# A graph layer on one core: a column cleared behind every gather, and the narrow one-hots of the edge count made by ScalarE

## The chip, the cores and the metric

One core of one Trainium2 chip runs the kernel. Its engines are TensorE (PE, with weight loads PEld), VectorE (DVE), ScalarE (ACT), GpSimd (POOL) and SyncE (SP). The metric is the device time of one execution in microseconds; the median of several executions is compared. The profile is of one further execution.

## The reference, cut to what matters

6250 nodes with 256 features, 200,000 edges sorted by destination. The part that the change touches is the sum over edges.

```
h_neigh  = xn @ W_neigh
h_sparse = _maxk(h_neigh, 32)                 # keeps the 32 largest of a row
msg      = h_sparse[src]                      # a gather of 200,000 rows
summed   = segment_sum(msg, dst)              # added up by destination
deg      = segment_sum(ones, dst)
neigh    = summed / maximum(deg, 1)
gnn      = xn @ W_self + neigh
x        = x + gnn + mix(xn)                  # mix: linear attention with a gate
x        = x + ffn(layernorm(x))              # on the half of the rows with the largest weight
```

The layer norm, the attention, the gate and the closing network over the chosen rows are in the kernel too and are the same before and after.

## The kernel before

Nodes are cut into 50 tiles of 125. All engines' programs are written out by hand, joined by semaphores alone; nothing is scheduled by a tool. After a first stage (projection, the 32 largest, softmax sums; to about 266 us) comes the loop of 50 positions, one per tile of destinations, in an order set by a table `ORDER` before the program is built.

**Gathered tiles.** For 41 of the tiles GpSimd gathers the source rows of each edge from DRAM (`rows_d`, 512 fp16 each) with indirect DMAs of 128 rows. Four make a group, and `ring` holds eight groups; 232 groups make 928 gathers. Before a group GpSimd waits until PE has freed the slot (`s_slot_free`); SyncE waits for each group to land and tells PE (`s_landed`, line 588). For each group DVE makes a one-hot of destinations (line 1445), and PE adds the rows up with four matmuls of 512 columns and four of 2 (`visit`, lines 1057 and 1058).

**Dense tiles.** The first nine tiles have most edges. For them the kernel counts how often each pair of source and destination occurs, and then multiplies the count by the whole table (lines 1104, 1105). The count is taken in windows of ten destinations, 117 windows in all, and each window in units of at most 16 chunks of 128 edges. A chunk takes two one-hots on DVE, both by comparing `iota` with a column: a narrow one `lo` of 125 (the source within its tile, line 1461) and a wide one `key` of 500 (source tile and destination, line 1462). PE multiplies the two and adds up in one of two banks (line 1044); ACT takes a finished window out (line 874, "evacuation"). 978 chunks are counted, spread over the gathered tiles' positions, always at a position's end. Both one-hots lie in `count_hot`, 16 slots; `s_hot` tells that a chunk is made, `s_hot_free` and `s_counts` that PE has read it.

**A position, engine by engine.** PE: gate and projection matmuls, the visits, then `count` of its units. DVE: destination one-hots, `row_chain` of the position before (21 short steps), the count's one-hots, then sums. ACT: loads, `stage` (lines 821 and 822: it copies a unit's columns to `lo_staged` and `key_staged`), the gate's tanh (`gate_open`, line 812), the evacuations, the gate's gelu, stores. PE may not begin a window before ACT has emptied its bank:

```
if unit.first and unit.window >= 2:
    pe.wait_ge(s_evac, unit.window - 1)
```

`hold(engine, semaphore, value)` is a wait with an increment of a semaphore that nobody waits for.

## Time and profile before

| what | value |
|---|---|
| median of 3 runs | 2366.26 us (2359.95 to 2393.0) |
| the profiled execution, its own time | 2391.38 us |
| its span, first to last instruction | 2389.2 us |
| mean granted TensorE clock | 0.769 |
| busy | PE 1505.8, DVE 1297.9, ACT 288.7, POOL 1116.1 us |
| first and last gather | 266.1 and 2126.1 us |

A busy time counts an engine once however many instructions overlap. Idle time before a group of instructions is put down to what ended it; "remote" there, and "another core or an unknown queue" in the chain, mean that a semaphore was updated at a time at which no instruction of the profile ended. "issue" means that the engine waited for nothing that the profile shows.

### The profile page before, as it was taken

How to read it: one execution, taken by the hardware profiler on the slowest of the kernel's cores; microseconds unless marked ns; L12 is line 12 of the kernel's file. 1: busy time of each engine (PE TensorE's matmuls, PEld its weight loads, DVE VectorE, ACT ScalarE, POOL GpSimd, SP SyncE). 2: the span in 40 equal slices, each digit the busy share in tenths (PEclk: the TensorE clock that was granted, in tenths of full speed). 3: DMA queues.
4: the chain of work that ended last, by engine and by line, in shares of the span. 5: the costliest groups of instructions: out<-in, count | busy, mean ns of one | idle time of the engine just before them, and what ended most of it. 6: DMA issues, size and time to landing. Idle time of an engine off the chain costs nothing.

```text
span 2389.2 us, 29676 instructions
## 1 busy us (share of the span) xinstructions
PE 1505.8 (63%) x6995; PEld 945.6 (40%) x6995; DVE 1297.9 (54%) x4748; ACT 288.7 (12%) x764; POOL 1116.1 (47%) x1260
## 2 busy tenths in 40 slices
PE   2996545546655655765375666484748577653998
PEld 0553432223422422442243344352425354442666
DVE  6999624446754455555346546474555657475111
ACT  1443200000000000100001001011111111100211
POOL 2455646554656345445523644545353555342312
PEclk8998766667866776777677777786878677875999
DMA  8221333343433222323322322323232332231201
GB/s 172 67 77 60 111 91 102 84 112 95 124 86 96 65 78 85 90 65 87 91 64 75 95 80 79 100 76 89 72 91 78 88 111 72 81 91 47 71 18 29
DMA packets 128612, 199.87 MB, mean 84 GB/s; under 512 B 37596, under 2 KB 89643, under 8 KB 128510
## 3 DMA queue, kind: packets, MB, share of 16 engines
q0 software_dynamic: 53616, 131.54, 19.5%
q10 hardware_dynamic: 45176, 47.09, 7.3%
q1 hardware_dynamic: 29718, 20.03, 3.7%
q8 instruction: 45, 0.74, 0.1%
q14 instruction: 57, 0.47, 0.1%
HBM read 162.33 MB, written 35.71 MB: 83 GB/s over the span
## 4 chain that ended last, share of the span: by engine, by line
PE 30%; another core or an unknown queue 22%; DVE 21%; issue 18%; DVEq 3%; ACTq 2%; ACT 2%; SPq 1%; DMA 1%; POOL 0%; POOLq 0%
PE bank L1104 6%; DVE region_k L1462 5%; PE bank L1044 5%; DVE region_k L1461 5%; PE bank L1151 4%; PE bank L1165 3%; PE bank L1057 3%; PE bank L958 1%; PE bank L1030 1%; DVEq L1445 1%; ACTq L464 1%; DVE region_r L1346 1%; PE bank L1033 1%; DVE region_r L1342 1%
## 5 line engine op out<-in xcount | busy, mean ns | idle before, releaser
L719 POOL DMA_INDIRECT ring<-rows_d,stage x928 | 928.8, 1001 | 935.8 <-PE bank L1057 632.8
L1044 PE MATMUL bank<-region_k 128*125 128x500 f16 x978 | 407.9, 515 | 536.1 <-issue 216.8
L1461 DVE TENSOR_SCALAR region_k<-iota,region_k 128x125 f16<-128x125 f16 x978 | 281.6, 288 | 475.9 <-remote 408.2
L1044 PEld LDWEIGHTS bank<-region_k 128*125 128x125 f16 x978 | 156.8, 168 | 771.1 <-issue 352.0
L1462 DVE TENSOR_SCALAR region_k<-iota,region_k 128x500 f16<-128x500 f16 x978 | 350.9, 359 | 18.2 <-issue 17.8
L1057 PE MATMUL bank<-ring,region_v 128*125 x1084 | 315.2, 416 | 43.4 <-issue 43.3
L1445 DVE SCALAR_TENSOR_TENSOR region_v<-iota,tile_start,dstT 128x500 f16 x271 | 198.3, 740 | 77.6 <-issue 34.2
L874 ACT ACTIVATE region_k<-bank 125x500 f16<-125x500 f32 (+1 forms) x117 | 65.8, 578 | 1127.6 <-remote 852.6
L1057 PEld LDWEIGHTS bank<-ring,region_v 128*125 x1084 | 150.4, 139 | 126.8 <-issue 47.6
L1058 PE MATMUL bank<-ones,region_v 128*125 128x2 f16 x1084 | 182.4, 168 | 18.2 <-issue 17.7
L1058 PEld LDWEIGHTS bank<-ones,region_v 128*125 x1084 | 152.5, 141 | 29.7 <-issue 29.7
L1104 PE MATMUL bank<-region_r,region_k 125*125 125x512 f16 x450 | 140.7, 441 | 16.2 <-issue 16.2
L958 PE MATMUL bank<-region_r 128*125 128x512 f32 x200 | 96.7, 606 | 0.0
L1104 PEld LDWEIGHTS bank<-region_r,region_k 125*125 125x125 f16 x450 | 66.8, 148 | 54.9 <-issue 25.0
L1151 PE MATMUL bank<-region_k,region_v 128*128 128x500 f32 (+1 forms) x224 | 87.2, 548 | 1.4 <-DVE region_k L1670 1.4
L1165 PE MATMUL bank<-region_v,region_k 128*125 128x256 f32 x400 | 87.3, 379 | 0.0
L743 POOL DMA_INDIRECT out_dram<-region_r,region_v x24 | 28.6, 1190 | 125.8 <-DVE region_r L1690 122.1
L1105 PE MATMUL bank<-ones,region_k 125*125 125x2 f16 x450 | 77.4, 172 | 9.7 <-issue 9.6
L1165 PEld LDWEIGHTS bank<-region_v,region_k 128*125 128x125 f32 x400 | 74.6, 188 | 10.9
L691 POOL CAST region_r<-region_r 125x256 f16<-125x256 f32 x50 | 25.1, 502 | 114.3 <-DVE region_r L1350 112.7
L1553 DVE TENSOR_SCALAR col_deg<-bank 125x1 f32<-125x1 f32 x50 | 7.7, 154 | 129.7 <-PE bank L1109 112.4
L1030 PE MATMUL bank<-region_v 128*125 128x256 f32 x200 | 75.4, 513 | 0.0
(307 smaller groups left out, 1988.8 us busy)
## 6 DMA issues: line engine op xcount, KB each, us to landing
ring<-rows_d,stage POOLq DMA_INDIRECT x928
kept_d<-region_v ACTq DMA_DIRECT2D x50, 252.0 KB
region_v<-xT_d ACTq DMA_DIRECT2D x53, 125.0 KB
xT_d<-region_r ACTq DMA_DIRECT2D x51, 125.0 KB, 2.0
rows_d<-region_r SPq DMA_DIRECT2D x50, 125.0 KB
region_k<-in_x_dram ACTq DMA_DIRECT2D x50, 125.0 KB
out_dram<-region_v ACTq DMA_DIRECT2D x50, 125.0 KB
region_v<-in_x_dram SPq DMA_DIRECT2D x5, 1120.0 KB
```

Of the source, the lines that this page charges most:

```text
L719: pool.indirect_dma_start(out=ring[:, c, :], out_offset=None, in_=rows_d, in_offset=bass.IndirectOffsetOnAxis(ap=stage[:, c:c + 1], axis=0 ...
L958: m = pe.matmul(bank[1 + s % 2][0:T, :], xT[:, s % 2, k * T:(k + 1) * T], wkv[:, k, :], start=(k == 0), stop=(k == KC - 1))
L1030: pe.matmul(p_sum, xTc[:, turn, k * T:(k + 1) * T], w_self[:, k, :], start=(k == 0), stop=False)
L1044: m = pe.matmul(out, lo, key, start=(c == WINDOW_AT[unit.window]), stop=(c + 1 == WINDOW_AT[unit.window + 1]))
L1057: m = pe.matmul(total, onehot_s, row_s, start=False, stop=False, skip_group_check=True)
L1058: d = pe.matmul(deg_sum, onehot_s, ones16[:], start=False, stop=False, skip_group_check=True)
L1104: pe.matmul(total, counts16[:, b, :], table[:, b, :], start=False, stop=False, skip_group_check=True)
L1151: m = pe.matmul(up_bank(n)[:, 0:wide], w1[:, k, n * 128:(n + 1) * 128], x3T[:, g % 2, k, 0:wide], start=(k == 0), stop=(k == KC - 1))
L1165: m = pe.matmul(y_pair(h)[:, u % 2, :], hid[:, g % 2, n, u * T:(u + 1) * T], w2[:, n, :], start=(n == 0), stop=(n == NH - 1))
L1445: dve.scalar_tensor_tensor(out=part(hot_bytes, HOT, SLOT_HOT, hot, 0, SLOT_HOT).bitcast(F16).rearrange("p (a t) -> p a t", a=GC), in0=iota ...
L1461: dve.tensor_scalar(lo, iota[:, 0:T], lo_staged[:, at, u:u + 1], None, ALU.is_equal)
L1462: dve.tensor_scalar(key, iota[:, 0:KEYS], key_staged[:, at, u:u + 1], None, ALU.is_equal).then_inc(s_hot, 1)
```

## The change

It has two parts.

1. Behind every gather GpSimd sets one column of a new small tile `pause` to zero. The last clear of a group raises `s_pause`, and before each round of eight groups GpSimd waits for the clears of the round before.
2. The narrow one-hot is no longer made by DVE. ACT makes it in two steps: |iota - lo| per chunk (Abs with the negated column as bias), and Relu(1 - that) over up to eight chunks (`PIECE`) at once, in place, after a wait for its own Abs (`s_far`). `s_lo` tells PE. The narrow ones get 32 slots (`lo_hot`), the wide ones 12 (`key_hot`).

With the second part ACT's order changes: staging stands behind the gate's tanh and is interleaved with the low halves, and the evacuation of a window behind the low halves of the next unit.

```diff
-    COUNT_HOT = 16
+    KEY_HOT = 12
+    LO_HOT = 32
+    PIECE = 8
...
+    PIECES_OF = []
+    for unit in UNITS:
+        before = sum(len(pieces) for pieces in PIECES_OF)
+        PIECES_OF.append([Piece(before + p, unit.at + offset, min(PIECE, unit.chunks - offset))
+                          for p, offset in enumerate(range(0, unit.chunks, PIECE))])
...
+        pause = sb("pause", [128, RING * GC])
...
+            pool.sem_inc(s_pause, 1)
...
                         done = (r + BLOCKS[block][0]) * ROUNDS + j
+                        hold(pool, s_pause, done * RING + 1)
...
                                     in_offset=bass.IndirectOffsetOnAxis(ap=stage[:, c:c + 1], axis=0)).then_inc(s_land[block][q], 16)
+                                paused = pool.memset(pause[:, c:c + 1], 0.0)
+                            paused.then_inc(s_pause, 1)
...
-                act.activation(lo_staged[:, unit.number % STAGED, 0:unit.chunks], src_lo[:, bass.ds(at, unit.chunks)], ACT.Copy)
+                act.activation(lo_staged[:, unit.number % STAGED, 0:unit.chunks], src_lo[:, bass.ds(at, unit.chunks)], ACT.Copy,
+                               scale=-1.0)
...
+            def low(unit):
+
+                act.wait_ge(s_staged, unit.number + 1)
+                for piece in PIECES_OF[unit.number]:
+                    if piece.at + piece.chunks > LO_HOT:
+                        free(act, piece.at + piece.chunks - 1 - LO_HOT)
+                    for c in range(piece.at, piece.at + piece.chunks):
+                        last = act.activation(lo_slots(c), iota[:, 0:T].rearrange("p (a t) -> p a t", a=1), ACT.Abs,
+                                              bias=lo_staged[:, unit.number % STAGED, c - unit.at:c - unit.at + 1])
+                    last.then_inc(s_far, 1)
+                    act.wait_ge(s_far, piece.number + 1)
+                    ends = min(piece.chunks, LO_HOT - piece.at % LO_HOT)
+                    for first, chunks in ((piece.at, ends), (piece.at + ends, piece.chunks - ends)):
+                        if chunks:
+                            last = act.activation(lo_slots(first, chunks), lo_slots(first, chunks), ACT.Relu, bias=ones[:, 0:1],
+                                                  scale=-1.0)
+                    last.then_inc(s_lo, 1)
...
+                act.wait_ge(s_m3, n + 2)
+                gate_open(n + 1)
+                closed = []
                 for unit in at.units:
                     stage(unit)
-                act.wait_ge(s_m3, n + 2)
-                gate_open(n + 1)
...
+                    low(unit)
+                    while closed:
+                        evacuate(closed.pop(0))
                     if unit.last:
...
+                        closed.append(unit.window)
+                while closed:
+                    evacuate(closed.pop(0))
...
-                    lo, key = hot_slot(c)
+                    if c == unit.at or PIECE_OF[c] != PIECE_OF[c - 1]:
+                        pe.wait_ge(s_lo, PIECE_OF[c] + 1)
                     pe.wait_ge(s_hot, c + 1)
...
-                    if c >= COUNT_HOT:
-                        free(c - COUNT_HOT)
-                    dve.tensor_scalar(lo, iota[:, 0:T], lo_staged[:, at, u:u + 1], None, ALU.is_equal)
-                    dve.tensor_scalar(key, iota[:, 0:KEYS], key_staged[:, at, u:u + 1], None, ALU.is_equal).then_inc(s_hot, 1)
+                    if c >= KEY_HOT:
+                        free(dve, c - KEY_HOT)
+                    dve.tensor_scalar(key_slot(c), iota[:, 0:KEYS], key_staged[:, at, u:u + 1], None, ALU.is_equal).then_inc(s_hot, 1)
```

The order on GpSimd before, at the head of a round of the gathers:

```order
L708 ISA
L176 ISA [waits s_slot_free]
L719 DMA ring<-rows_d,stage 128x512 [waits s_stage0]
L719 DMA ring<-rows_d,stage 128x512 x3
L176 REGISTER_ALU
L719 DMA ring<-rows_d,stage 128x512 [waits s_slot_free]
```

and the same place now:

```order
L734 ISA
L186 ISA [waits s_pause,s_slot_free]
L746 DMA ring<-rows_d,stage 128x512 [waits s_stage0]
L749 MEMSET pause 128x1
L746 DMA ring<-rows_d,stage 128x512
L749 MEMSET pause 128x1
```

Each of the four gathers of a group has a memset behind it, and the head of a round waits for `s_pause` as well as for the slot.

On ACT before, the staging of the last of three units of a position, the gate's tanh (L812) and the three evacuations:

```order
L821 ISA [waits s_hot]
L821 ACTIVATE region_k<-region_k 128x6
L822 ISA
L822 ACTIVATE region_k<-region_k,win_start 128x6
L812 ACTIVATE region_v<-bank 128x250 [waits s_m3]
L874 ACTIVATE region_k<-bank 125x50x10 [waits s_counts] x2
L874 ACTIVATE region_k<-bank 125x50x5 [waits s_counts]
L809 ACTIVATE hgT<-region_v,bg 64x125 [waits s_hgpre]
```

and now the same position from its tanh (L841) through the low halves of its first unit, of nine chunks; L850 and L852 stage, L862 is the Abs and L869 the Relu:

```order
L841 ACTIVATE region_v<-bank 128x250 [waits s_m3]
L477 TENSOR_LOAD bounds
L477 ISA x2
L850 ISA [waits s_hot]
L850 ACTIVATE region_k<-region_k 128x9
L852 ISA
L852 ACTIVATE region_k<-region_k,win_start 128x9
L862 ACTIVATE region_k<-iota,region_k 128x125 [waits s_hot_free,s_staged]
L862 ACTIVATE region_k<-iota,region_k 128x125 x7
L869 ACTIVATE region_k<-region_k,ones 128x8x125 [waits s_far]
```

The tanh has moved ahead of all staging, and a unit's staging, Abs and Relu now stand together; the evacuation of its window comes only behind those of the next unit.

On DVE before, the end of `row_chain` and the first chunks of the count:

```order
L1516 TENSOR_SCALAR w_all<-col_w,br 125x1 [waits s_step5]
L1517 TENSOR_SCALAR region_v<-col_w,br 125x1
L1461 TENSOR_SCALAR region_k<-iota,region_k 128x125 [waits s_step6,s_hot_free,s_staged]
L1462 TENSOR_SCALAR region_k<-iota,region_k 128x500
L1461 TENSOR_SCALAR region_k<-iota,region_k 128x125 [waits s_hot_free]
```

and now:

```order
L1562 TENSOR_SCALAR w_all<-col_w,br 125x1 [waits s_step5]
L1563 TENSOR_SCALAR region_v<-col_w,br 125x1
L1516 TENSOR_SCALAR region_k<-iota,region_k 128x500 [waits s_step6,s_hot_free,s_staged]
L1516 TENSOR_SCALAR region_k<-iota,region_k 128x500 [waits s_counts]
L1516 TENSOR_SCALAR region_k<-iota,region_k 128x500 [waits s_hot_free] x7
```

Only the wide one-hots are left, each with its wait for a free slot. In the built program ACT has 978 Abs and 183 Relu more, DVE 978 one-hots less.

## Rows read from the trace of the kernel before

**Rows 1.** The page: busy time of each engine, and the chain by engine.

```profile
PE 1505.8 (63%) x6995; PEld 945.6 (40%) x6995; DVE 1297.9 (54%) x4748; ACT 288.7 (12%) x764; POOL 1116.1 (47%) x1260
...
PE 30%; another core or an unknown queue 22%; DVE 21%; issue 18%; DVEq 3%; ACTq 2%; ACT 2%; SPq 1%; DMA 1%; POOL 0%; POOLq 0%
```

**Rows 2.** The page's costliest groups: busy us, mean ns, then idle time before and releaser.

```profile
L719 POOL DMA_INDIRECT ring<-rows_d,stage x928 | 928.8, 1001 | 935.8 <-PE bank L1057 632.8
L1044 PE MATMUL bank<-region_k 128*125 128x500 f16 x978 | 407.9, 515 | 536.1 <-issue 216.8
L1461 DVE TENSOR_SCALAR region_k<-iota,region_k 128x125 f16<-128x125 f16 x978 | 281.6, 288 | 475.9 <-remote 408.2
...
L874 ACT ACTIVATE region_k<-bank 125x500 f16<-125x500 f32 (+1 forms) x117 | 65.8, 578 | 1127.6 <-remote 852.6 <-PE bank L1044 204.7 <-issue 70.3
```

**Rows 3.** Busy time by stretch: PE, PEld, DVE, ACT, POOL, granted clock, DMA share, GB/s.

```profile
1318.30:1327.70 9.40, 5.42 (x16) 1.75 (x14) 6.94 (x29) 0.00 (x0) 7.27 (x8) 0.80 0.36 99
1327.70:1338.10 10.40, 1.29 (x3) 0.36 (x2) 0.00 (x0) 0.00 (x0) 7.91 (x9) 0.50 0.37 109
1338.10:1341.40 3.30, 0.00 (x0) 0.00 (x0) 0.00 (x0) 0.00 (x0) 0.00 (x0) 0.50 0.14 40
```

**Rows 4.** Timeline around that burst: start, us, engine, instruction, [idle before <-releaser].

```profile
1314.48 0.21 ACT L821 ACTIVATE region_k<-region_k 128x7 f32 x1 [0.35 <-issue]
...
1318.38 1.90 PE L1044 MATMUL bank<-region_k 128*125 128x500 f16 x5
...
1326.44 0.57 PE L1044 MATMUL bank<-region_k 128*125 128x500 f16 x1 [1.10 <-DVE region_k L1462]
...
1330.68 0.57 PE L1044 MATMUL bank<-region_k 128*125 128x500 f16 x1 [0.83 <-issue]
...
1337.11 0.94 POOL L719 DMA_INDIRECT ring<-rows_d,stage  x1 [0.30 <-issue]
...
1341.41 0.26 DVE L1461 TENSOR_SCALAR region_k<-iota,region_k 128x125 f16<-128x125 f16 x1 [13.77 <-remote]
1341.61 1.07 ACT L874 ACTIVATE region_k<-bank 125x500 f16<-125x500 f32 x2 [26.46 <-remote]
1342.26 3.18 PE L1044 MATMUL bank<-region_k 128*125 128x500 f16 x7 [11.00 <-ACT region_k L874]
```

**Rows 5.** Busy time by stretch, columns as in rows 3: three other stretches with gathers.

```profile
585.80:590.80 5.00, 5.00 (x13) 2.08 (x12) 5.00 (x25) 0.59 (x1) 4.12 (x3) 0.57 0.29 80
...
633.90:640.80 6.90, 6.66 (x28) 3.60 (x26) 6.90 (x32) 0.59 (x1) 5.39 (x5) 0.96 0.34 99
1583.10:1593.20 10.10, 7.59 (x25) 3.93 (x24) 10.10 (x49) 2.95 (x5) 8.30 (x6) 0.82 0.28 78
```

**Rows 6.** Timeline of PE and POOL in the first two of these stretches.

```profile
584.51 11.82 PE L1044 MATMUL bank<-region_k 128*125 128x500 f16 x28 [2.35 <-DVE region_k L1462]
585.76 1.39 POOL L719 DMA_INDIRECT ring<-rows_d,stage  x1 [0.30 <-issue]
587.46 1.39 POOL L719 DMA_INDIRECT ring<-rows_d,stage  x1 [0.31 <-issue]
...
631.81 9.78 PE L1044 MATMUL bank<-region_k 128*125 128x500 f16 x33
```

**Rows 7.** Timeline of POOL at the start: memsets behind a DMA and among memsets.

```profile
6.61 0.57 POOL L643 DMA_DIRECT2D br<-in_L_ffn_br_dram  x1
7.16 0.24 POOL L644 MEMSET ident<- 128x128 f32 x1
...
11.22 0.09 POOL L666 MEMSET eps<- 125x1 f32 x1
```

**Rows 8.** Line 719, the gathers: ns least/median/most, first and last start.

```profile
L719 POOL DMA_INDIRECT ring<-rows_d,stage x928: 940/947/1717, 266.1 to 2126.1; - x186
```

**Rows 9.** ACT's groups from 400 to 2130 us: busy us, mean ns, idle before.

```profile
L822 ACT ACTIVATE region_k<-region_k,win_start 128x6 f32 (+10 forms) x123 | 35.7, 290 | 0.4 <-issue 0.4
...
L812 ACT ACTIVATE region_v<-bank 128x250 f32<-128x250 f32 x49 | 18.1, 370 | 183.5 <-PE bank L1025 114.7 <-remote 63.0 <-issue 5.7
```

More of the change, by code:

```diff
@@ L127, in build @@
             UNITS.append(Unit(len(UNITS), w, offset, held, WINDOW_AT[w] + offset, offset == 0, offset + held == chunks))
+    Piece = namedtuple("Piece", "number at chunks")
+    PIECES_OF = []
[3 more added lines that the diff above has]
+                          for p, offset in enumerate(range(0, unit.chunks, PIECE))])
+    PIECE_OF = {c: piece.number for pieces in PIECES_OF for piece in pieces for c in range(piece.at, piece.at + piece.chunks)}
     Spot = namedtuple("Spot", "dense tile units since")
@@ L214, in build @@
         counts16 = region_k.take([T, NT, T + 1], F16)[:, :, 0:T]
-        count_hot = region_k.take([128, COUNT_HOT, LW + KEYS], F16)
+        lo_hot = region_k.take([128, LO_HOT, LW], F16)
+        key_hot = region_k.take([128, KEY_HOT, KEYS], F16)
         lo_staged = region_k.take([128, STAGED, UNIT])
@@ L515, in agg_bank, with lo_slots, key_slot, free @@
             return bank[(0, 4)[at.n % 2]][0:T, :]
-        def hot_slot(c):
-            return count_hot[:, c % COUNT_HOT, 0:T], count_hot[:, c % COUNT_HOT, LW:LW + KEYS]
+        def lo_slots(c, chunks=1):
+            return lo_hot[:, c % LO_HOT:c % LO_HOT + chunks, 0:T]
+        def key_slot(c):
+            return key_hot[:, c % KEY_HOT, :]
+        def free(engine, c):
+            closed = sum(c >= end - 1 for end in WINDOW_AT[1:])
+            if c + 1 in WINDOW_AT:
+                engine.wait_ge(s_counts, closed)
+            else:
+                engine.wait_ge(s_hot_free, c + 1 - closed)
         def h_psum(s):
@@ L854, in store_row, with evacuate @@
                 act.dma_start(out_t[:, at.tile:at.tile + 1, :], rowbuf[:, u:u + 1, C:2 * C]).then_inc(s_rowout[u], 16)
+            def evacuate(window):
+                k = window % NW
+                wide = min(WIN, T - k * WIN)
+                act.wait_ge(s_counts, window + 1)
+                act.activation(counts16[:, :, k * WIN:k * WIN + wide],
+                               count_bank(window).rearrange("p (d h) -> p h d", h=NT)[:, :, 0:wide], ACT.Copy).then_inc(s_evac, 1)
             def position(at):
@@ L1041, in count @@
                 for c in range(unit.at, unit.at + unit.chunks):
-                    lo, key = hot_slot(c)
+                    if c == unit.at or PIECE_OF[c] != PIECE_OF[c - 1]:
+                        pe.wait_ge(s_lo, PIECE_OF[c] + 1)
                     pe.wait_ge(s_hot, c + 1)
-                    m = pe.matmul(out, lo, key, start=(c == WINDOW_AT[unit.window]), stop=(c + 1 == WINDOW_AT[unit.window + 1]))
+                    m = pe.matmul(out, lo_hot[:, c % LO_HOT, 0:T], key_slot(c), start=(c == WINDOW_AT[unit.window]), stop=(c + 1 == WINDOW_AT[unit.window + 1]))
                     m.then_inc(s_counts if c + 1 == WINDOW_AT[unit.window + 1] else s_hot_free, 1)
```

17 lines of the change are left out of this document (2 added, 15 removed).

## Prediction, made before the changed kernel had run

> **What bounds the kernel now.** I read the page's totals and chain first [rows 1]. No engine is full: PE is busy 63% of 2389.2 us, DVE 54%, POOL 47%. The chain that ended last is put down to "another core or an unknown queue" for 22% and to "issue" for 18%, although this kernel has one core. So two fifths of the path are waits that no finished instruction explains, and the question is where they lie.
>
> The costliest groups say where [rows 2]. PE sits idle 536.1 us before the 978 count matmuls (L1044), DVE 475.9 us before the 978 narrow one-hots (L1461), nearly all of it "remote", and ACT 1127.6 us before the 117 evacuations (L874). POOL sits idle 632.8 us before its gathers for PE to free a ring slot. All four wait for each other in the count phase.
>
> One position shows how. A burst of some 20 gathers runs from 1312.6 to 1338.1 [rows 3, 4]. From 1327.7 to 1338.1 PE is busy 1.29 of 10.4 us, DVE and ACT not at all, and only POOL works; for another 3.3 us after the burst nothing works. The single instructions are plainer [rows 4]: PE ends its 14th count at 1331.25, so the window whose seven chunks came first was complete long before, yet ACT starts its two evacuations at 1341.61 and DVE its next one-hot at 1341.41, both "remote". Finished work is told late. What coincides is the gathers, issued one behind the other with 0.30 us between: 0.95 + 0.30 = 1.25 us each.
>
> Other stretches have gathers and no such silence [rows 5, 6]. At 585.76 gathers of 1.39 us start 1.70 apart, and PE runs 28 counts without a gap (11.82 us). From 1583.1 to 1593.2, six gathers in 10.1 us, DVE is busy all the time and PE 7.59 us. From 633.9 to 640.8, five gathers in 6.9 us or 1.38 each, PE is busy 6.66 us, in a run of 33 counts. But from 1318.3 to 1327.7 [rows 3], eight gathers begin in 9.4 us (1.25 to 1.39 apart), and PE already waits up to 1.10 us for a one-hot long made [rows 4]. So signals pass freely at 1.7 us, hardly at 1.25, and either way in between. Cause and effect are not separable here: the longer gathers are also those beside which DVE works.
>
> **The clears.** Each of 928 gathers gets a memset of one column behind it. The nearest row is the 125x1 memset: 0.09 us, and a memset started 0.02 us before the POOL DMA ahead of it ended, without a gap of its own [rows 7]. So 928 x 0.09 = 84 us on POOL. It lies on the path as far as the burst does, which I take as all of it. The lower bound is 0, where POOL waits for a slot anyway (632.8 us [rows 2]). The upper bound is a second 0.30 us gap behind each clear: 928 x 0.39 = 362 us. I take 84, since the row of a memset behind a DMA is the nearest. The new wait on the clears stands once per 32 gathers, 28 times after the first; the group's gathers are queued behind it, then SP's forwarding of landings and PE's visits. If the clear's own signal is prompt it costs the drained queue, some 1 us, between 0 and the 3.3 us that signals took after the burst [rows 3]: 28 us, at most 92.
>
> What the clears give back is the disputed term. They part two gathers by 1.25 + 0.09 = 1.34 us at least, between the bad and the good stretch. Bounds: nothing, or all 536.1 us of PE's idle time before counts [rows 2]. I take half, 268 us.
>
> **The narrow one-hots.** DVE loses 978 instructions of 288 ns, 281.6 us [rows 2]. DVE is idle in the stalls, so this gives nothing by itself while the stalls stand; what it gives is less traffic beside the gathers. Those have median 947 and mean 1001 ns [rows 2, 8], so 928 x 54 ns = 50 us is stretch by DVE's work. With one of two one-hots gone I take half of it back, 25 us (bounds 0 and 50). The Trainium skill, "SBUF — State Buffer", section "Who interferes with whom", says that a DVE instruction in a two-port mode and a GpSimd instruction exclude each other for their whole length and that no other pair contends. The trace agrees on the first half (gathers of 1.39 beside one-hots, 0.95 alone); the second half leaves the late signals unexplained.
>
> ACT gains 978 Abs of 128x125 and 183 Relu, in the built program, of up to 8x125. Its nearest rows [rows 2, 9]: 290 ns for six elements with a bias column, 370 ns for 250 and 578 ns for 500 elements, so 208 / 250 = 0.83 ns an element. An Abs lasts 290 + 119 x 0.83 = 389 ns; two evacuations took 1.07 us together [rows 4] where one lasts 0.58 to 0.59, so 0.11 overlaps and the pitch is 0.28 us: 274 us. The Relus: 978 x 125 x 0.83 ns = 101 us, and 183 x 0.2 = 37 us to start. Together 412 us, 0.42 us a chunk. PE counts at 0.42 us a chunk (11.82 us for 28) at a granted clock of 0.57, near the lower of its levels, and at 0.30 (9.78 us for 33) at 0.96 [rows 5, 6]. In the 10 us of visits ACT runs ahead by up to 32 chunks, so at the low clock the low halves cost nothing. If PE no longer stalls and the clock stays high, ACT sets the pace: up to 978 x 0.12 = 117 us, which is the lid on a full release; I put none of it on the half release. ACT also waits for itself before each group of Relus; that wait and the signal to PE are two more that can come late. "ScalarE: Activation LUTs", section "Rules for kernel authors", of the Trainium skill speaks against this move (Relu and simple arithmetic belong on VectorE) and gives 0.3 us plus 0.83 ns an element: an estimate by it is 978 x 0.404 + 183 x 0.3 + 101 = 551 us. The trace agrees on the slope. ACT was busy 288.7 us of 2389.2, so either sum fits.
>
> The stages now stand behind the tanh of the gate, and each behind the low halves of the unit before. DVE's wide one-hots of the second unit thus wait some 7 x 0.42 = 2.9 us more, while PE counts the first. Key slots go from 16 to 12; PE had counted 14 when it stopped [rows 4], so DVE stops two chunks earlier in a stall. An evacuation stands behind the next unit's low halves; PE needs it only a unit later. I cost all three at nothing under the cover of the visits and of the first unit's counts; without it, 2.9 us in each of some 40 counting positions is 116 us, the reason why I take half and not more.
>
> **The sum** against the profiled execution (2391.38 us around a span of 2389.2): -268 + 84 + 28 - 25 = -181, so 2210. That execution lies 25 us over the median of 2366.26, so 2185; I say 2190.
>
> **The rivals.** *Full release.* Nothing comes late any more: 2391 - 536 + 84 + 28 - 25 + 117 = 2059, in the median 2034. POOL is no obstacle: 928 x 1.34 = 1244 us against the 1860 us from its first gather to its last [rows 8]. For it: 28 and 33 counts without a gap beside gathers. Against: the trace's good stretches are all ones in which DVE works without pause.
>
> *Slower: the burst only gets longer.* Signals hang on the gathers being in flight, not on the distance at which POOL issues them; the silence lasted 3.3 us beyond the last gather [rows 3], which a gap on POOL does not explain. Then each burst of some 20 grows by 20 x 0.09 = 1.8 us, and behind each come the same 3.3 us. Price: 84 + 28 us, and up to 2 us of late self-waits of ACT per position, about 20 us: 2391 + 132 = 2523, in the median 2498; with the Relus' signals hidden 2478. It decides if PE still stands idle 10 us before an evacuation.
>
> *No difference: the lock alone.* The distance at which gathers pass signals is set by DVE's work beside them, and the clears only make up for the one-hots taken away: 84 + 28 - 50 = +62, less some 60 us of stalls that 1.34 instead of 1.25 us relieves: 2391 + 2, in the median 2368. The row for it is the stretch from 1318.3 to 1327.7 [rows 3]. The skill's port rule, read strictly, gives this case.
>
> *The change does not do what it says* is thin: nobody reads the cleared tile, but the memset occupies POOL all the same.
>
> **Chances.** Half release (2090 to 2315) 0.42; full release (below 2090) 0.15; no difference (2320 to 2413) 0.16; slower 0.27. 2% of 2366 is 47 us, about what a measurement can tell from nothing; so faster 0.57, same 0.16, slower 0.27. The range leaves out the lower half of the full release and the tail of the slower case: 2035 to 2480.
>
> **What would show it.** In the new profile: (1) starts of gathers 1.34 us apart in bursts when DVE is idle; 1.6 or more means a second gap. (2) PE's idle time before counts, 536 now, near 270; near zero is the full release, unchanged the slower case. (3) "remote" ahead of the evacuations and of DVE's one-hots halved. (4) ACT's Abs near 0.39 us, in pitch 0.28, ACT busy near 700 us. (5) Mean gather below 1001 ns. (6) POOL's wait for PE (632.8) shrunk: whoever is late next is POOL itself, or ACT's low halves ahead of PE's counts. The forecast is wrong if the distance between gathers has nothing to do with the late signals, or if a clear costs far more than a memset among memsets.

## The result and the profile after

The changed kernel takes 2498.17 us in the median of four runs (2469.2 to 2519.12); the kernel before took 2369.61 us in four runs beside it. The ratio is 1.047, interval 1.039 to 1.055. It is below the ratio of the two medians (1.054) since it leaves out executions over 1.5% longer than the fastest of their kernel; the one profiled here, and those profiled in e3, e8 and e16 below, are of that kind. Forecast were 2190 us and a range of 2035 to 2480: the wrong direction, and the median is 18 us outside the range. The profiled execution took 2519.12 us around a span of 2517.1.

The page of the changed kernel: totals, the chain by engine, and the costliest groups (busy, mean ns of one, then the engine's idle time before them and what ended most of it).

```profile
span 2517.1 us, 30984 instructions
PE 1446.7 (57%) x6995; PEld 941.7 (37%) x6995; DVE 1145.0 (45%) x3770; ACT 732.5 (29%) x1925; POOL 1189.7 (47%) x2188
...
PE 31%; another core or an unknown queue 27%; DVE 15%; issue 14%; ACT 8%; DVEq 3%; SPq 1%; ACTq 1%; DMA 0%; POOL 0%; POOLq 0%
...
L746 POOL DMA_INDIRECT ring<-rows_d,stage x928 | 891.4, 961 | 985.4 <-PE bank L1113 756.1
L1100 PE MATMUL bank<-region_k 128*125 128x500 f16 x978 | 365.9, 507 | 757.0 <-ACT region_k L869 262.2
L1516 DVE TENSOR_SCALAR region_k<-iota,region_k 128x500 f16<-128x500 f16 x978 | 297.2, 373 | 805.6 <-remote 415.9
...
L862 ACT ACTIVATE region_k<-iota,region_k 128x125 f16<-128x125 f16 x978 | 300.5, 388 | 60.5 <-PE bank L1100 56.4
L908 ACT ACTIVATE region_k<-bank 125x500 f16<-125x500 f32 (+1 forms) x117 | 66.4, 571 | 850.1 <-remote 691.7
...
L869 ACT ACTIVATE region_k<-region_k,ones 128x1000 f16<-128x1000 f16 (+7 forms) x183 | 153.7, 853 | 5.5 <-ACT region_k L862 0.3
...
L749 POOL MEMSET pause<- 128x1 f32 x928 | 115.5, 124 | 0.3
```

Against [rows 1, 2]: PE's idle time before the counts (L1044, now L1100) rose from 536.1 to 757.0 us, the wait of the gathers for PE from 632.8 to 756.1, and the unexplained share of the chain from 22 to 27%. The mean gather fell from 1001 to 961 ns. The clears (L749) cost POOL 115.5 us of busy time. The view of line L746 gives the first and last start; before they were 266.1 and 2126.1 [rows 8]:

```profile
L746 POOL DMA_INDIRECT ring<-rows_d,stage x928: 940/946/1719, 265.7 to 2249.3; - x186
```

The gathering stretch is 124 us longer, the rest of the program 4 us. One burst of it in the timeline of all engines (start, length, engine, line, tiles, and in brackets the idle time ahead of it):

```profile
1380.78 0.95 POOL L746 DMA_INDIRECT ring<-rows_d,stage  x1 [0.19 <-issue]
...
1381.71 0.12 POOL L749 MEMSET pause<- 128x1 f32 x1
1381.97 0.58 PE L1088 MATMUL bank<-region_v 128*125 128x256 f32 x1 [1.50 <-issue]
1382.03 0.95 POOL L746 DMA_INDIRECT ring<-rows_d,stage  x1 [0.19 <-issue]
1382.97 0.12 POOL L749 MEMSET pause<- 128x1 f32 x1
1383.28 0.94 POOL L746 DMA_INDIRECT ring<-rows_d,stage  x1 [0.19 <-issue]
...
1384.07 0.58 PE L1088 MATMUL bank<-region_v 128*125 128x256 f32 x1 [1.51 <-issue]
...
1389.00 0.37 PE L1074 MATMUL bank<-region_v 128*128 128x125 f32 x1 [1.05 <-issue]
1390.41 0.95 POOL L746 DMA_INDIRECT ring<-rows_d,stage  x1 [0.19 <-issue]
1391.10 0.37 PE L1074 MATMUL bank<-region_v 128*128 128x125 f32 x1 [1.74 <-issue]
...
1393.99 0.16 DVE L1599 TENSOR_SCALAR col_deg<-bank 125x1 f32<-125x1 f32 x1 [20.01 <-remote]
...
1394.23 0.59 ACT L908 ACTIVATE region_k<-bank 125x500 f16<-125x500 f32 x1 [23.14 <-remote]
```

Three things stand here. Gathers start 1.25 us apart (1380.78, 1382.03, 1383.28), just as before: the gap of 0.30 us is now 0.12 us of clear and 0.19 of rest. And the silence is the same: DVE waits 20.01 us and ScalarE 23.14 us, until 3 us behind the last gather, while PE starts one matmul in 1.4 to 2.1 us. And the matmuls that PE starts so slowly have no wait in the program between them (L1088 twice, then L1074): late signals of other engines can't hold them. A count over the whole trace says the same of matmuls that follow one of their own line with no wait between: from the seventh distance on in a row of gathers (each begun under 1.30 us after the last) PE stands idle 284 ns before them on average (61 matmuls), elsewhere 6 ns (1785). So "finished work is told late" is a part of what happens: PE's own next step can be late as well. The windows of the same burst show it in sums (us, busy time of each engine, granted clock):

```profile
1382.00:1391.40 9.40, 2.75 (x6) 1.43 (x5) 0.00 (x0) 0.00 (x0) 7.34 (x14) 0.50 0.36 99
```

DVE and ACT do nothing in 9.4 us, PE is busy 2.75 us of them at the lower level of its clock (0.50). New is a wait inside the count phase, in the view of waits of DVE (in all, times, longest):

```profile
DVE region_k L1516 <- remote: 415.9, 24, 36.1
DVE region_k L1516 <- ACT region_k L852: 222.4, 38, 25.1
```

In the kernel before DVE waited 7.5 us for the same staging. PE's waits before the counts changed hands, too. Before and after:

```profile
PE bank L1044 <- ACT region_k L874: 161.0, 14, 21.2
PE bank L1044 <- DVE region_k L1462: 131.4, 101, 19.1
```
```profile
PE bank L1100 <- ACT region_k L869: 262.2, 21, 25.4
PE bank L1100 <- DVE region_k L1516: 257.8, 35, 29.5
```

PE no longer waits for an evacuation (the wait for L874 has no counterpart for L908), but for the Relus that make the narrow one-hots, and twice as long for the wide ones.

### The profile page after: what moved, and what is told of

It reads as the page before. It is cut to its first block, busy times and chain, and to the rows that moved or that the text cites. A ratio compares the mean times of both kernels' runs of the same rounds, so it can differ in the third digit from the quotient of the medians.

```text
span 2517.1 us, 30984 instructions
## 1 busy us (share of the span) xinstructions
PE 1446.7 (57%) x6995; PEld 941.7 (37%) x6995; DVE 1145.0 (45%) x3770; ACT 732.5 (29%) x1925; POOL 1189.7 (47%) x2188
## 4 chain that ended last, share of the span: by engine, by line
PE 31%; another core or an unknown queue 27%; DVE 15%; issue 14%; ACT 8%; DVEq 3%; SPq 1%; ACTq 1%; DMA 0%; POOL 0%; POOLq 0%
PE bank L1100 6%; PE bank L1160 5%; DVE region_k L1516 4%; ACT region_k L862 4%; PE bank L1207 3%; PE bank L1221 3%; PE bank L1113 3%; PE bank L1085 2%; ACT region_k L869 2%; PE bank L1074 1%; PE bank L1013 1%; PE bank L1088 1%; PE bank L1068 1%; DVEq L1501 1%
## 5 line engine op out<-in xcount | busy, mean ns | idle before, releaser
L746 POOL DMA_INDIRECT ring<-rows_d,stage x928 | 891.4, 961 | 985.4 <-PE bank L1113 756.1
L1100 PE MATMUL bank<-region_k 128*125 128x500 f16 x978 | 365.9, 507 | 757.0 <-ACT region_k L869 262.2
L1516 DVE TENSOR_SCALAR region_k<-iota,region_k 128x500 f16<-128x500 f16 x978 | 297.2, 373 | 805.6 <-remote 415.9
L1100 PEld LDWEIGHTS bank<-region_k 128*125 128x125 f16 x978 | 160.2, 173 | 940.8 <-issue 610.6
L862 ACT ACTIVATE region_k<-iota,region_k 128x125 f16<-128x125 f16 x978 | 300.5, 388 | 60.5 <-PE bank L1100 56.4
L908 ACT ACTIVATE region_k<-bank 125x500 f16<-125x500 f32 (+1 forms) x117 | 66.4, 571 | 850.1 <-remote 691.7
L869 ACT ACTIVATE region_k<-region_k,ones 128x1000 f16<-128x1000 f16 (+7 forms) x183 | 153.7, 853 | 5.5 <-ACT region_k L862 0.3
L749 POOL MEMSET pause<- 128x1 f32 x928 | 115.5, 124 | 0.3
L841 ACT ACTIVATE region_v<-bank 128x250 f32<-128x250 f32 x51 | 19.3, 379 | 310.2 <-PE bank L1080 257.1
```

The source lines that it names most:

```text
L746: pool.indirect_dma_start(out=ring[:, c, :], out_offset=None, in_=rows_d, in_offset=bass.IndirectOffsetOnAxis(ap=stage[:, c:c + 1], axis=0 ...
L862: last = act.activation(lo_slots(c), iota[:, 0:T].rearrange("p (a t) -> p a t", a=1), ACT.Abs, bias=lo_staged[:, unit.number % STAGED, c - ...
L869: last = act.activation(lo_slots(first, chunks), lo_slots(first, chunks), ACT.Relu, bias=ones[:, 0:1], scale=-1.0)
L1100: m = pe.matmul(out, lo_hot[:, c % LO_HOT, 0:T], key_slot(c), start=(c == WINDOW_AT[unit.window]), stop=(c + 1 == WINDOW_AT[unit.window + 1]))
L1516: dve.tensor_scalar(key_slot(c), iota[:, 0:KEYS], key_staged[:, at, u:u + 1], None, ALU.is_equal).then_inc(s_hot, 1)
```

## The experiments

Every ratio is to the kernel before, timed on the same chip (its medians were 2371 to 2421 us). The first four expectations name times for a chip on which it takes 2370; theirs took 2421, so I compare ratios. I add a count worked out from the starts of the 928 gathers in each trace: how many times eight gathers in a row began within 9.0 us. I call this a **close train**, counted anew from every gather, so a long row holds several; the kernel before has 250, the changed one 402 in the profile above. Seven distances of over 1.29 us can't make a close train, so for five and ten clears the 0 only repeats that gathers start 1.33 or 1.47 us apart.

| kernel | ratio [95%] | PE idle before counts, us | close trains |
|---|---|---|---|
| one clear (e1) | 0.988 [0.979, 0.996] | 523.1 | 226 |
| low halves on ScalarE, no clear (e2, e16) | 1.026 [1.017, 1.035]; 1.049 [1.032, 1.065] | 633.0; 719.2 | 483; 506 |
| ScalarE's staging late (e3) | 1.002 [0.994, 1.011] | 576.7 | 283 |
| five clears (e4) | 0.871 [0.865, 0.878] | 132.5 | 0 |
| the changed kernel (e5, e17) | 1.052 [1.041, 1.062]; 1.058 [1.047, 1.069] | 697.3; 722.7 | 400; 395 |
| changed, staging early (e6) | 1.032 [1.022, 1.041] | 685.6 | 364 |
| changed, five clears (e7) | 0.904 [0.896, 0.911] | 277.8 | 0 |
| three clears (e8) | 0.937 [0.927, 0.947] | 408.1 | 69 |
| changed, five clears, no Relu (e9) | 0.894 [0.887, 0.901] | 258.6 | 0 |
| ten clears (e10) | 0.875 [0.871, 0.879] | 30.8 | 0 |
| changed, five clears, staging early (e11) | 0.893 [0.888, 0.898] | 253.3 | 0 |
| five increments (e12) | 0.877 [0.872, 0.881] | 109.8 | 60 |
| ten increments (e13) | 0.896 [0.888, 0.905] | 10.4 | 0 |
| five waits (e14) | 1.020 [1.008, 1.033] | 587.2 | 249 |
| twenty increments a group (e15) | 0.880 [0.873, 0.886] | 95.0 | 64 |
| eleven waits (e18) | 0.878 [0.874, 0.883] | 105.4 | 65 |

### The parts of the change alone

**One clear.** The kernel before with `pause`, `s_pause`, the wait at the head of a round and

```
                                    in_offset=...).then_inc(s_land[block][q], 16)
+                                paused = pool.memset(pause[:, c:c + 1], 0.0)
+                            paused.then_inc(s_pause, 1)
```

> The kernel before with the clears behind the gathers and the wait on them once a round; both one-hots stay on DVE. Theory A (the clears are innocent: in the profile after, gathers still started 1.25 us apart, so each clear of 0.12 us lies inside the gap of 0.30 us that was there before): 2340 to 2395, gathers 1.25 apart, PE idle before the counts some 536 us as before. Rival B (the clears cost a gap of their own or their wait does, and are the loss): 2450 to 2500. Rival C (the clears do free the signals, as forecast, and ScalarE's part ate more than they gave): under 2300, PE idle before the counts under 450 us.

Measured 0.988: theory A, with gathers still 1.25 us apart. The clear and its wait cost nothing on balance and give 1.2%.

**The low halves alone.** The changed kernel without the lines above.

> The changed kernel without the clears and their wait; ScalarE makes the narrow one-hots. Theory A (all of the loss is in ScalarE's part): 2465 to 2530, PE idle before the counts some 750 us. Rival B (the clears are the loss): near 2370. Rival C (the clears helped and ScalarE's part cost more than the loss seen): above 2530.

Measured 1.026, half of the loss at first sight. A later comparison moved that (below).

**The order alone.** In `position` of the kernel before:

```
-                for unit in at.units:
-                    stage(unit)
                 act.wait_ge(s_m3, n + 2)
                 gate_open(n + 1)
+                for unit in at.units:
+                    stage(unit)
```

> The kernel before with one thing of the change: ScalarE stages the indices of a position's units behind the gate's tanh instead of ahead of the wait for the projection. No clears, DVE makes both one-hots. Theory A1 (ScalarE's staging now comes late, and DVE's one-hots with it: in the profile after DVE stands idle 222 us for the staging, in 38 stretches): a good part of the loss, 2420 to 2490, and DVE idle for the staging some 150 us or more. Theory A2 (the loss is in the extra signals and work of the low halves, not in the order): 2350 to 2390, since DVE has other work until then.

Measured 1.002, and DVE waits 9.3 us for the staging: A2. Behind the tanh alone it comes in time.

**Both parts, and the staging put back.** The changed kernel again, and the changed kernel with `stage` of all units ahead of `act.wait_ge(s_m3, n + 2)` and only `low` behind it.

> The changed kernel once more, on the chip of the three beside it, since chips differ by 2% (before took 2370 on one, 2421 on another). By the ratios so far of the two parts alone (clears 0.988, ScalarE's low halves 1.026) the sum of both would be 1.014, by the first comparison 1.047. Theory A (the parts add up): ratio 1.00 to 1.03. Rival B (the clears' gift is lost when ScalarE makes the low halves, or turns into a loss): 1.035 to 1.055.

> The changed kernel with the staging of all units of a position put back ahead of the wait for the projection, as in the kernel before. Theory A (what the move to ScalarE costs is that each unit's wide one-hots wait for a staging behind the low halves of the unit before, 222 us of DVE's idle time): DVE idle for the staging falls below 60 us and the ratio to before is 1.00 or less. Rival B (the stall only changes its name: DVE would wait for its slots, which come free late as well, since gathers still start 1.25 us apart): within 1% of the changed kernel.

1.052 and 1.032 on one chip; the first is in its rival B's range. DVE's wait for the staging was 204.6 us in the first and 2.3 us in the second; its "remote" wait before the same one-hots rose from 357.6 to 614.6. So neither held in full: theory A's wait went, but its ratio of 1.00 did not come, and 2% is more than rival B's 1%. Of 205 us only some 50 us of time came back (2502 to 2453); the rest of the stall changed its name, as B has it. What makes the staging late is not the tanh alone (e3); what is left are the low halves of the unit before, which stand ahead of it and wait themselves.

**With and without the clear on one chip.**

> ScalarE's low halves without the clears, once more, now on one chip with the changed kernel. Theory A (the two parts add up: low halves +2.6 to +5%, one clear -1.2%): the ratio is that of the changed kernel or above, 1.04 to 1.065. Rival B (with ScalarE's part in place one clear makes it worse): 1.015 to 1.035, clearly under the changed kernel's.

> The changed kernel a third time, beside the one without clears, on one chip. Both theories expect 1.04 to 1.06 as in the two comparisons so far; what tells them apart is its distance to the run without clears: 0 to 0.02 below it (A), or 0.02 or more above it (B).

1.049 without and 1.058 with it; the intervals overlap, and 0.009 above is neither theory's distance. Whether the one clear does any harm there is not settled; no gift of it shows. ScalarE's part carries the loss.

### What frees the signals

**Five clears, three, ten.** In place of the one memset,

```
+                                for m in range(5):
+                                    paused = pool.memset(pause[:, c * 5 + m:c * 5 + m + 1], 0.0)
```

and likewise with 3 and 10 (with 10, `pause` is of fp16).

> The kernel before with five clears of one column behind each gather, and the wait on them once a round. By 0.12 us a clear, of which 0.30 us fit in the gap, gathers should start some 1.55 to 1.7 us apart in a burst. Theory D (signals come late when gathers follow closely, and a distance of about 1.7 us frees them, as in the good stretches of the kernel before): PE idle before the counts falls from 536 to under 300 us, 2150 to 2330. Rival E (what counts is that gathers are in flight or queued, not how far apart they start): the bursts get longer by 20 x 0.4 us a position and nothing is given back, 2450 to 2700.

> The kernel before with three clears behind each gather. A clear behind another adds some 0.03 us (five took 0.23 us together), so three should take 0.17 us, and the next gather should start 1.25 to 1.28 us after the last. Theory D (what frees the signals is any distance over 1.25 us): ratio between 0.87 and 0.99, and near 0.99 if gathers still start 1.25 apart. Rival E (what frees them is the number of small instructions between two gathers, whatever the distance): half way between one clear (0.988) and five (0.871), near 0.93, with gathers 1.25 apart.

> The kernel before with ten clears behind each gather. By 0.035 us a clear the next gather starts 0.95 + 0.40 + 0.15 = 1.50 us after the last. If what frees the signals is used up at 1.33 us (PE's idle time before the counts is down to 132 us of 536), five more clears only lengthen the bursts: 928 x 0.17 = 158 us on POOL, which waits 340 us anyway, so 0.86 to 0.90. If more signals pass the more there is between two gathers, it goes on falling: 0.80 to 0.85.

Five clears gave 0.871, three 0.937, ten 0.875. The timeline of POOL with five:

```profile
1320.92 0.95 POOL L723 DMA_INDIRECT ring<-rows_d,stage  x1 [0.15 <-issue]
1321.87 0.23 POOL L727 MEMSET pause<- 128x1 f32 x5
1322.25 0.97 POOL L723 DMA_INDIRECT ring<-rows_d,stage  x1 [0.15 <-issue]
```

Starts are 1.33 us apart, not the 1.55 to 1.7 expected, and that is enough. It is the distance that the prediction had put down for one clear. PE's idle time before the counts is down to 132.5 us, so three quarters of the 536 went and not the half, and 311 us of the time are gone. The page of the same run:

```profile
L723 POOL DMA_INDIRECT ring<-rows_d,stage x928 | 955.1, 1029 | 339.6 <-PE bank L1064 165.6
...
L1051 PE MATMUL bank<-region_k 128*125 128x500 f16 x978 | 343.7, 469 | 132.5 <-issue 68.0
```

The busy time of the counts fell as well, from 407.9 to 343.7 us, at a granted clock of 0.807 over the run (0.769 before).

With three clears gathers start 1.27 us apart in most rows. At 0.937 that fits both expectations, so it doesn't tell the distance from the number of instructions. With ten clears gathers start 1.47 us apart, PE's idle time is 30.8 us, and the chain is POOL's own:

```profile
POOL 48%; PE 20%; issue 15%; DVE 9%; DMA 3%; another core or an unknown queue 2%; DVEq 1%; SPq 1%; POOLq 1%; ACTq 0%; ACT 0%
```

So ten clears take away nearly all of PE's wait and give it back in longer bursts. That fits the expectation's first case.

**Instructions that never reach the engine.** Five increments of a semaphore that nobody waits for, behind each gather; then ten:

```
+                                for m in range(5):
+                                    pool.sem_inc(s_alone, 1)
```

> The kernel before with five increments of a semaphore that nobody waits for behind each gather, in place of clears: instructions of POOL's sequencer alone, 0.02 us each in the trace. Theory D (distance is what counts): the effect follows the starts of the gathers; if they are 1.25 us apart as before, 0.99 to 1.01; if 1.33, near 0.87. Rival E (instructions of the engine itself, each with its end, let signals through): no effect at any distance. Rival F (more signals on POOL's own queue make it worse): over 1.02.

> The kernel before with ten increments of the unread semaphore behind each gather. Five gave 0.877 while gathers still started 1.25 us apart (eight of them from 1315.3 to 1325.0, with PE busy all of the 9.7 us), so distance is not what frees the signals. Theory G (the number of instructions of POOL's stream between two gathers is, about 2.6% each as with one, three and five clears, until the stalls are used up): 0.84 to 0.875. Rival H (five is enough for all there was, and more only fill POOL's sequencer at some 0.08 us each): 0.875 to 0.90.

0.877 and 0.896. Rivals E and F of the first fall, and theory D, read by the single distance, as well; the second is in rival H's range. With five, single gathers still start 1.25 us apart. POOL's timeline shows what differs:

```profile
1321.53 0.95 POOL L719 DMA_INDIRECT ring<-rows_d,stage  x1 [0.30 <-issue]
1322.78 0.95 POOL L719 DMA_INDIRECT ring<-rows_d,stage  x1 [0.30 <-issue]
1324.04 0.95 POOL L719 DMA_INDIRECT ring<-rows_d,stage  x1 [0.30 <-issue]
1326.03 0.94 POOL L719 DMA_INDIRECT ring<-rows_d,stage  x1 [1.05 <-issue]
1328.94 0.94 POOL L719 DMA_INDIRECT ring<-rows_d,stage  x1 [1.97 <-issue]
```

The train breaks, since the engine waits for its sequencer. The second expectation took this stretch for a proof that distance does not matter, PE being busy throughout it (9.70 of 9.7 us). It proves less: the stretch lies at the start of a row, and PE runs there the dense multiplication (L1106), whose operands were ready. Over the whole trace close trains fell from 250 to 60. Ten increments leave none, but now the sequencer sets the pace: POOL's idle time for "issue" is 599.4 us and for PE 36.3.

**Which instructions, and where.** Five satisfied waits on a setup semaphore; eleven of them; twenty increments behind the fourth gather of each group and none between:

```
+                                for m in range(5):        # 11 in the second
+                                    pool.wait_ge(s_setup, SETUP)
```

> The kernel before with five waits behind each gather for a semaphore that reached its value in the setup, in place of increments: instructions of POOL's sequencer that neither run on the engine nor write a semaphore. Theory G (any instruction between two gathers counts): 0.86 to 0.90. Rival I (it is the writing of a semaphore, or an end of an instruction, that lets the others' signals through): 0.99 to 1.01. If the five are built into one instruction, G expects about 0.97.

> The kernel before with eleven satisfied waits behind each gather. Five were built into two instructions of POOL's sequencer and one wait on the gather, and gave 1.020; eleven should make five instructions, as many as the five increments (0.877), 0.09 us each, that write nothing. Theory G (the number of instructions between two gathers decides, or the time that the sequencer spends on them): 0.87 to 0.92. Rival I (instructions that write nothing do not count; increments and the clears' ends do): 0.98 to 1.03.

> The kernel before with twenty increments behind the fourth gather of each group, and none between the four: as many as with five behind each. Theory K (what counts is that every gather is parted from the next by them): three of four gathers follow closely as before, and the ratio is 0.94 to 1.0. Rival L (the number of increments in all, or the 1.6 us that they take on POOL's sequencer per group, decides): 0.87 to 0.91, with a gap of about 1 us behind each fourth gather.

Five waits gave 1.020, eleven 0.878, twenty increments a group 0.880. In the traces waits go in pairs: five became two instructions of the sequencer a gather, eleven became five. Five waits missed both expectations: 2% slower than the kernel before and clear of it, which I can't explain. With eleven theory G holds, and rival I falls (instructions that write nothing do it too, if there are five). L holds of the place, though the next gather starts only 0.3 us later behind a fourth (1.56 us in the median), not 1 us. The waits of POOL for itself ("issue": in all, times, longest), in the kernel before, with five waits and with eleven:

```profile
POOL ring L719 <- issue: 265.6, 858, 1.7
```
```profile
POOL ring L719 <- issue: 281.7, 867, 3.6
```
```profile
POOL ring L719 <- issue: 384.6, 888, 3.0
```

Two instructions a gather hardly change this wait and leave 249 close trains; five add 119 us of gaps of the engine, leave 65 trains, and take 290 us off the whole. Over all kernels with both one-hots on DVE the ratio follows the trains: 226 to 283 of them, 0.99 to 1.02; 60 to 69, 0.88 to 0.94; none, 0.87 to 0.90. Among the kernels with ScalarE's part and at most one clear it doesn't: the two without the clear have the most trains (483 and 506) and ratios no higher (1.026 and 1.049) than those with it (395 and 400; 1.058 and 1.052).

### What ScalarE's part costs once signals flow

> The changed kernel with five clears behind each gather in place of one, so that gathers start 1.33 us apart at least, as with five clears in the kernel before (2110 against 2421, where PE's idle time before the counts fell from 536 to 132 us). Theory A (late signals are most of the loss, and ScalarE's low halves by themselves cost little once signals flow): ratio to before 0.85 to 0.89. Rival B (ScalarE, at 0.42 us a chunk, then sets the pace and holds its other work back): 0.90 to 0.96, with PE's idle time before the counts put down to ScalarE's Relu.

> The changed kernel with five clears, without the 183 Relus and ScalarE's wait for itself ahead of them; the narrow halves then hold |iota - lo| in place of the one-hot, so the edge counts are not those of the reference. With the Relus the ratio to before was 0.904, and PE stood 86 us before counts for the Relu. Theory A (ScalarE's pace in the count phase, 0.31 us an Abs and 0.16 us a chunk of Relu, is what its part costs): 153.7 us of Relu go, and the ratio falls to 0.86 to 0.885, near that of five clears with both one-hots on DVE (0.871). Rival B (the cost is the order on ScalarE and its signals, whatever its work): 0.895 to 0.91.

> The changed kernel with five clears in place of one, and with the staging back ahead of the wait for the projection. The staging behind the tanh cost 2% in the changed kernel (1.052 against 1.032). Theory A (with signals flowing it costs the same, since the second unit's staging stands behind the first's low halves in either): 0.88 to 0.895 against 0.904. Rival B (with signals flowing the staging comes in time): 0.90 to 0.91.

The changed kernel with five clears gave 0.904, at the lower edge of rival B's range, with an interval that reaches below it; PE's wait for the Relu is there, but a third of its idle time before the counts. Five clears with both one-hots on DVE had given 0.871. Without the Relus (L863 to L870 of that kernel; the narrow halves then hold a distance, not a one-hot) it was 0.894, with the staging early 0.893 (theory A of that run). Both were timed on another chip than the 0.904, and the intervals overlap, so 1% is about what this can tell. The waits of PE with five clears, and with the Relus away:

```profile
PE bank L1101 <- issue: 157.8, 67, 13.9
...
PE bank L1101 <- ACT region_k L870: 86.2, 19, 10.3
```
```profile
L1094 PE MATMUL bank<-region_k 128*125 128x500 f16 x978 | 328.2, 486 | 258.6 <-DVE region_k L1510 152.9
```

PE's wait of 86 us for the Relu becomes one of 153 us for DVE; its idle time before the counts hardly moves (277.8 to 258.6). So the Relus are a small part at most; the 978 Abs stood in every run (PE waited 63.3 us for them without the Relus), so ScalarE's pace in them is not tested. Against 0.871 a cost of 3.3 points is left, 2.2 with the staging early, that I did not take apart further.

## Why the prediction was wrong

Two steps failed. The clear was to set gathers 1.34 us apart and so give back 268 us for 112; it left them at 1.25 and measured -28 us. And ScalarE's part, costed at nothing with a gain of 25 us, measured 2.6 and 4.9%, 61 to 116 us of 2366. Forecast and result (-181 and +111 us) are 292 us apart, and these two make 214 to 297 of them: the clear 128, or 156 if it gives nothing beside ScalarE's part, the low halves 86 to 141.

**What bounds the kernel.** Right in the main. Rows of gathers that follow closely are the cause of the silence: with five clears, changed in nothing but GpSimd's stream, PE's idle time before the counts fell from 536 to 132.5 us. That all of it is finished work told late was too narrow, since PE's matmuls without a wait stood late too.

**The clears: the step that failed.** The prediction put the clear on top of the gap ("1.25 + 0.09 = 1.34 us at least"). It lies inside it: 0.12 us of clear in 0.30 us of gap, starts 1.25 us apart. So the +84 us didn't show, the +28 us for the wait neither, and with them went the -268 us, whose condition was the distance. The prediction had weighed a second gap behind the clear (362 us) but not that the first gap was there for the taking; its own row of a memset that began 0.02 us before the DMA ahead of it ended [rows 7] pointed there. One clear measured 0.988, -28 us in place of -156. Given the distance, the half release was too small: at 1.33 us apart 311 us went, where half less the cost of the clears makes 156 and all less that cost 424.

**The gather stretch: the sign.** The one-hots taken from DVE did shorten the gathers, from 1001 to 961 ns, more than the 27 ns forecast (my -25 us). But no run shows it as a gain. In the kernel before a gather beside DVE's work lasted longer and began 1.38 us after the last [rows 5]. Without the narrow one-hots, gathers begun under 1.30 us after the last went from 624 to 787 of 927, close trains from 250 to 402 (483 and 506 without the clear), and the silence with them. The prediction had both halves, that the long gathers are those beside DVE's work and that they let signals through, and named it in the rival "the lock alone", which set +62 us for clears and lost stretch against -60 us of stalls. With no distance from the clear only the loss was left. This link rests on the counts, and they don't bear it out among themselves, since the kernels with most trains are not the slowest; no run gave DVE other work in place of the one-hots. So it is argued and not shown.

**The narrow one-hots on ScalarE.** The sizes were right: Abs 388 ns (389 forecast), seven of them in 2.14 us, which is 0.29 apart (0.28), Relus 153.7 us (138), ACT busy 732.5 (700). "Cost at nothing" was wrong: without clears it is 2.6 to 4.9%, and with five clears still 3.3 points. What it lacked are the hand-overs: PE stood 262.2 us for the Relus and 257.8 for the wide one-hots, where it had waited 161.0 for evacuations and 131.4 for DVE. The Trainium skill, "ScalarE: Activation LUTs", section "Rules for kernel authors", keeps Relu and simple arithmetic off ScalarE because VectorE is faster per element. Its durations agree (0.3 + 125 x 0.83 ns = 404 ns against 388); the advice came out right, yet not for its reason, since taking the Relus away altogether gave 1% at most that shows (0.904 to 0.894, intervals overlapping).

**The order.** Of the three edits cost at nothing, one was not covered: each staging now stands behind the low halves of the unit before, and DVE waited 222.4 us in 38 stretches, 5.9 us each where the prediction said 2.9. Put back, it gives 2% (e6). Behind the tanh alone it costs nothing (e3), as forecast. The smaller key ring and the later evacuations were not tried alone. The traces say of them that DVE's wait for PE to free a slot rose from 29.1 to 84.1 us, and PE's for an evacuation went from 161.0 us to nothing.

**The rivals.** The slower rival named 2478 to 2498, and 2498 was measured. That was luck: the distance of gathers did not grow by the clears, and its part for ScalarE's late waits was 20 us, where the whole loss lay. Of its sign, an idle PE before an evacuation, half is there: evacuations still come up to 37.8 us late, but no wait of PE is put down to them.

**The six signs.** Starts 1.34 apart: 1.25. PE's idle time near 270: 757. "Remote" halved: 852.6 to 691.7 for the evacuations, 408.2 to 415.9 for DVE. ACT: as forecast (0.388 us, 0.29 apart, 732.5 busy). Mean gather below 1001 ns: 961. The gathers' wait for PE shrunk: it grew to 756.1.

## What to carry to other kernels

An instruction that is meant to part two others parts them only by what does not fit into the gap that is there; read the pitch, not the instruction's length, and try the dose (one, three, five gave 1, 6 and 13%) before deciding that a remedy fails or works. Where finished work is told late, an operation moved to an idle engine adds hand-overs that can be late; that it also took away a contention which held the cause in check is argued here, not shown. The lowest ratio measured is that of the kernel before with five clears behind each gather: 2109.84 us against 2420.63 on its chip, 0.871. Ten clears, five increments and eleven waits are within 1% of it, too near to be told apart on different chips; the last two need no tile.

## What the runs showed of the hardware

In this kernel the other engines slow down along a row of gathers. In the kernel before, while each gather begins under 1.30 us after the last, PE is busy 0.65 of the time in the first three distances of a row (294 of them), 0.37 in the next three (147), then 0.19 (93) and 0.13 (55). With ten clears, gathers under 1.50 us apart, it stays at 0.68, 0.61, 0.54 and 0.60 (337, 110, 57, 37). The silence ends some 3 us after the last gather. I had not expected 0.08 us to decide over 300.

The distance alone is not it, though. With five increments it is 1.25 us inside a row, as before, yet PE's idle time before the counts is 109.8 us: rows of eight and more of such gathers went from 39 to 14. The trace's semaphore updates are no measure here, since many are not recorded singly: of 978 raises of `s_hot` it has 662 in the kernel before and 206 with ten clears.

The gathers' data do not back up. In the trace of the changed kernel the last packet of a row on the gathers' queue ends 1.47 us after GpSimd's last gather in 22 rows of nine gathers and more, and 1.46 us in 10 rows of four and fewer (medians; rows that no gather followed for 6 us).

A one-column clear behind a gather adds nothing to the distance of 1.25 us (0.12 us in a gap of 0.30); five together take 0.23 us and add 0.08.

POOL's sequencer shows the hold-up as well. An increment of it takes 17 ns in the median, but up to 1394 ns with five behind each gather:

```profile
L723 POOLq EVENT_SEMAPHORE  x4640: 2/17/1394, 266.3 to 1829.9; - x194
```

The Trainium skill, "SBUF — State Buffer", section "Who interferes with whom", lets only DVE and GpSimd exclude each other. The silence is no case of that rule: ScalarE stood 23.14 us in it, and PE's matmuls without a wait stood too; and eleven waits, which touch no tile, took most of it away (0.878). Open is what lets the engines go on: time between gathers, or that GpSimd's sequencer is no longer ahead of its engine. No run holds one and changes the other.
